# Making the stored copy of a turned tile on GpSimd instead of ScalarE, in a fused linear-attention and mixture-of-experts kernel

## The reference

```python
xn = _layernorm(x, axis=-1)
x = x + attn(xn) + ffn(xn)
# attn: q = xn@Wq, v = xn@Wv, s[t] = lam*s[t-1] + v[t], y = layernorm(q*s)*ln_g + ln_b
#       y = y * silu(xn@Wg), out = y@Wo
# ffn:  probs = softmax(xn@router.T), top 8 of 64 experts, at most 128 tokens an expert,
#       silu(xg@w1) * (xg@v1) @ w2, scaled by the weight and added to its tokens
```

## Time and profile before

| what | us |
|---|---|
| median of 3 runs | 2541.22 (2540.82 to 2541.46) |
| the profiled execution, its own time | 2539.86 |
| span of its trace | 2538.2 |
| PE busy | 2493.7 |
| DVE busy | 1629.1 |
| ACT busy | 1320.7 |
| POOL busy | 674.5 |

### The profile page before, as it was taken

One profiled execution on the slowest core, in us unless ns is written; L12 is line 12 of the kernel. 1 busy time (PEld: TensorE's weight loads), 2 busy tenths in 40 slices (PEclk: granted clock), 3 DMA queues, 4 the chain that ended last, 5 costly groups with the idle time before them and its releaser, 6 DMA issues.

```text
span 2538.2 us, 39295 instructions
## 1 busy us (share of the span) xinstructions
PE 2493.7 (98%) x13649; PEld 2214.3 (87%) x13649; DVE 1629.1 (64%) x1689; ACT 1320.7 (52%) x1499; POOL 674.5 (27%) x523
## 2 busy tenths in 40 slices
PE   7999999999999999999999999999999999999997
PEld 6888978898889988899888998889988889988896
DVE  7776897666666665666566666656666566656654
ACT  5566323554446644556445565445654456544554
POOL 3221122223322232322223222322223222323211
PEclk9999999999999999999999999999999999999999
DMA  8785854897668966779766797765986669866686
GB/s 278 260 301 193 240 189 162 257 306 228 191 224 254 312 215 217 228 234 295 239 228 204 227 316 249 224 217 197 311 277 191 224 217 284 276 217 228 207 268 162
DMA packets 151790, 605.74 MB, mean 239 GB/s; under 512 B 20592, under 2 KB 37040, under 8 KB 151216
## 3 DMA queue, kind: packets, MB, share of 16 engines
q1 hardware_dynamic: 116304, 518.91, 57.1%
q0 software_dynamic: 35424, 86.00, 16.5%
HBM read 520.89 MB, written 100.70 MB: 245 GB/s over the span
## 4 chain that ended last, share of the span: by engine, by line
PE 93%; DVE 3%; DMA 2%; ACT 1%; issue 1%; POOL 0%; SPq 0%; ACTq 0%; DVEq 0%; POOLq 0%
PE psA L1543 18%; PE psA L1545 18%; PE psA L1544 18%; PE psH L1543 7%; PE psH L1545 7%; PE psH L1544 7%; PE psY L1543 4%; PE psY L1545 4%; PE psY L1544 3%; PE psX L1650 2%; PE psY L1575 2%; PE psX L1670 1%; DMA ew_raw<-ew_dram 1%; DMA xn_turned<-xraw 1%; PE psH L1689 1%
## 5 line engine op out<-in xcount | busy, mean ns | idle before, releaser
L1156 DVE TENSOR_TENSOR ew_lo<-ew_raw,ew_hi 128x1536 fp32r<-128x1536 f32 x384 | 693.9, 1816 | 340.1 <-ACT ew_hi L752 326.0
L752 ACT ACTIVATE ew_hi<-ew_raw 128x1536 fp32r<-128x1536 f32 x384 | 568.4, 1484 | 163.0 <-DMA ew_raw<-ew_dram 128.5
L1543 PE MATMUL psA<-xT_hi,pw_hi 128*128 128x512 f32 (+1 forms) x1544 | 621.3, 402 | 3.5 <-DVE xT_lo L1073 2.9
L746 ACT ACTIVATE pw_hi<-pw_raw 128x1024 fp32r<-128x1024 f32 x254 | 266.4, 1060 | 674.2 <-PE psA L1545 671.7
L1545 PE MATMUL psA<-xT_hi,pw_lo 128*128 128x512 f32 (+1 forms) x1544 | 610.5, 395 | 0.0
L1544 PE MATMUL psA<-xT_lo,pw_hi 128*128 128x512 f32 (+1 forms) x1544 | 606.8, 393 | 0.0
L1151 DVE TENSOR_TENSOR pw_lo<-pw_raw,pw_hi 128x1024 fp32r<-128x1024 f32 x256 | 313.8, 1236 | 161.5 <-ACT pw_hi L746 156.1
L1543 PE MATMUL psH<-ew_hi,gT_hi 128*128 128x384 f32 x1024 | 352.7, 344 | 0.8
L1545 PEld LDWEIGHTS psA<-xT_hi,pw_lo 128*128 128x128 f32 x1544 | 292.4, 189 | 69.8
L1544 PEld LDWEIGHTS psA<-xT_lo,pw_hi 128*128 128x128 f32 x1544 | 294.9, 191 | 63.5
L1543 PEld LDWEIGHTS psA<-xT_hi,pw_hi 128*128 128x128 f32 x1544 | 291.5, 189 | 64.9 <-issue 4.7
(11 more groups left out here) (161 smaller groups left out, 3342.3 us busy)
## 6 DMA issues: line engine op xcount, KB each, us to landing
ew_raw<-ew_dram SPq DMA_DIRECT2D x384, 768.0 KB, 6.3
pw_raw<-proj_w_dram SPq DMA_DIRECT2D x256, 512.0 KB, 5.2
xn_scratch<-xt SPq DMA_DIRECT2D x33, 512.0 KB, 4.6
xt<-x_dram SPq DMA_DIRECT2D x32, 512.0 KB, 6.0
out_dram<-x_dram SPq DMA_DIRECT2D x32, 512.0 KB, 5.7
out_dram<-ot POOLq DMA_DIRECT2D x32, 512.0 KB, 12.4
xn<-xn_turned SPq DMA_DIRECT2D x29, 512.0 KB, 4.1
xn_turned<-xraw SPq DMA_DIRECT2D x28, 512.0 KB, 5.1
```

The lines of the kernel that those rows point to most:

```text
L746: act.activation(dst[:, slot, :, :], pw_raw[:, slot, :, :], ACT.Copy).then_inc(s_pwhi, 1)
L752: act.activation(ew_hi[:, c % 3, :], ew_raw[:, c % 3, :], ACT.Copy).then_inc(s_ewhi, 1)
L1156: dve.tensor_tensor(ew_lo[:, c % 3, :], ew_raw[:, c % 3, :], ew_hi[:, c % 3, :].bitcast(F32), ALU.subtract).then_inc(s_ewlo, 1)
L1543: pe.matmul(dst, l_hi, r_hi_, start=first, stop=False)
```

## The change

GpSimd gets `whole(k)`: it waits for `rt_lo` of tile k, and for the store of tile k-2, and adds the high and the low part into `xraw`. The raw copy on ACT is gone. `low` on DVE subtracts from the PSUM bank instead of `xraw`. The waits follow: ACT's rounded copy of tile k waits for the sum of tile k-2 (both read the same `rt_hi` buffer), and PE's turn of the last eight tiles waits for the low part of the tile before (the bank is read until then). The `z_lo` of block 0 and the sums of the last eight tiles alternate on GpSimd. SP's list is the same.

```diff
+            def whole(k):
+
+                if k >= NT + 2:
+                    wait_alone(pool, s_tst[k % 2], 16 * ((k - NT) // 2))
+                pool.wait_ge(s_plo, k + 1)
+                pool.tensor_tensor(xraw[:, k % 2, :, :], rt_hi[:, k % 2, :, :].bitcast(F32),
+                                   rt_lo[:, k % 2, :, :].bitcast(F32), ALU.add).then_inc(s_praw, 1)
...
                     if k % NT == 2:
                         inv_std(group_of(k) + 1)
+                    whole(k)
                 if p % 4 == 0 and p > 0:
                     add_sums(0, mm - 1, 1)
                 elif p % 4 == 2:
                     add_sums(0, mm, 0)
             add_sums(0, KC // 2 - 1, 1)
             inv_std_y(0)
-            inv_std(NB + 1)
-            for m in range(KC - 1):
-                z_lo_of(0, m)
+            for m in range(KC):
+                if m == 2:
+                    inv_std(NB + 1)
+                    z_lo_of(0, 0)
+                if m >= 2:
+                    z_lo_of(0, m - 1)
+                whole(NTILE - KC + m)
...
             def turned_hi(k):
                 act.wait_ge(s_pT, k + 1)
                 dst = xT_hi[:, :, k * P:(k + 1) * P] if k < NT else rt_hi[:, k % 2, :, :]
-                if k >= NT:
-                    if k >= NT + 2:
-                        wait_alone(act, s_tst[k % 2], 16 * ((k - NT) // 2))
-                    act.activation(xraw[:, k % 2, :, :], chunks(bank_of(k)), ACT.Copy).then_inc(s_praw, 1)
+                if k >= NT + 2:
+                    act.wait_ge(s_praw, k - NT - 1)
                 act.activation(dst, chunks(bank_of(k)), ACT.Copy).then_inc(s_phi, 1)
...
-                raw = chunks(bank_of(k)) if k < NT else xraw[:, k % 2, :, :]
-                dve.tensor_tensor(dst, raw, hi.bitcast(F32), ALU.subtract).then_inc(s_plo, 1)
+                dve.tensor_tensor(dst, chunks(bank_of(k)), hi.bitcast(F32), ALU.subtract).then_inc(s_plo, 1)
...
                 if k >= NTILE - KC:
-                    pe.wait_ge(s_phi, k)
-                    pe.wait_ge(s_plo, k - 1)
+                    pe.wait_ge(s_plo, k)
                 elif k >= NT:
                     pe.wait_ge(s_plo, k - 1)
```

## The result

| what | before | after |
|---|---|---|
| median of 20 runs each | 2537.66 us (2533.60 to 2541.95) | 2541.97 us (2538.66 to 2545.12) |
| profiled execution, its own time | 2539.86 | 2545.12 |
| span of its trace | 2538.2 | 2543.3 |

The ratio after to before is 1.0017, with a 95% interval of 1.0010 to 1.0024: 4.3 us longer, less than the 0.2% that was called no change. The forecast was 2545.2 us, range 2537.0 to 2550.0, and +4.0 us. It started from the median of three runs, 2541.22 us; over 20 runs the kernel before has 2537.66, so the forecast time is 3.2 us above the measured one although the difference is nearly right.

A forecast was written before the change was run, and what follows sets the result against it. PE, busy 98%, bounds the kernel; only idle gaps and low-clock stretches can be won. Terms +1.5 - 1.3 - 1.6 + 3.3 + 1.0 + 1.1 = +4.0 us on 2539.86, plus 1.36, give 2545.2 us, range 2537 to 2550.

The forecast's parts named there:

- The price of a sum: One GpSimd addition of 128x1024, 28 of them: 2.4 us each, 67 us in all, hidden as busy time.
- A: PE's 2.32 us idle gap before tile 8: whole(6) ahead of both sums costs 2.4, shorter chain gives 0.9, +1.5 us.
- B: PE's 1.29 us idle gap for `keys`: `keys` ready about 0.6 us before PE needs it, -1.3 us.
- C: PE's 1.62 us idle gap before tile 18: high part of tile 17 no longer waits for a store, -1.6 us.
- E: PE's 0.18 us idle gap before the token sums: whole(22), whole(23) and collisions delay them to about 188.6 us, +3.3 us.
- D: PE's 0.30 us idle gap at 176.6 us, which the prediction counted into E.
- F: PE's 2.10 and 1.38 us gaps at the stretch's end: 0.8 us won for k = 6, k = 7 later, +1.0 us.
- G: PE's 0.66 us idle gap at 339 us: last store issued later, DVE enters its saturated stretch late, +1.1 us.
- The clock: PE's granted clock in 20 us stretches: a 0.83 row costs 3.4 us; the sum of +4.0 us had only waiting.
- Rival two: "Another stretch at half clock" behind the late token sums: 3.4 us more, +7.4 us in all, 2548.6 us; chance 0.20.
- the locks miss: Rival: GpSimd and DVE collisions fall beside the chains; -7.6 us, 2533.6 us, or 2537.0 without the clock; chance 0.17.
- no change: Rival: what B and C give is what E and F take, the rest hidden; 2541.2 +- 1 us; chance 0.08.

The follow-up runs named there:

- Experiment 1: Changed kernel with GpSimd's whole(22) and whole(23) moved behind the last add_sums of the projections: 2533.17 us, ratio 0.9984 to the kernel before.
- experiment 3: Changed kernel with one wait more, GpSimd's whole(22) waiting for the nmr of tiles 24 to 27: 2540.64 us, ratio 1.0012 to the kernel before.
- experiment 5: Changed kernel with one wait more, GpSimd's whole(31) waiting for DVE's last low part lo_z7: 2543.81 us, ratio 1.0022 to the kernel before.
- experiment 2: Changed kernel with GpSimd's whole(6) moved behind rs and both add_sums of step p = 2, and waiting for nmr: 2536.19 us, ratio 0.9990.

## Why the prediction was right, and where it wasn't

**The verdict and the time held**, in part by luck: idle time rose by 2.2 us where the sum had +4.0, the clock, which the sum had at nothing, added some 4.6 us up to 280 us, and the two errors offset each other.

**The price of a sum** was 2.4 us on record and 2.40 in the trace. The guess by a memset's growth over size was good. The reading that two SBUF inputs exclude GpSimd held at every place named; it was too narrow, as the mask and the cast (one source) waited as well.

**A: +1.5 on record, +1.12 measured.** From the end of `rs` to the end of `nmr` the chain grew by 2.05 us (4.06 to 6.11), not 2.4: this half was off. The other half, 0.9 us from the copy that ACT no longer makes, was right, though `rs` came later, at 55.82 instead of 54.83 us. The low clock at the start had made everything late, PE too, which ran dry at 60.85 instead of 58.93 us. Against PE, `rs` is 0.93 us earlier, and 2.05 - 0.93 is the 1.12 us. In the kernels with the half sum and the copy, without that low clock, it came at 54.05 and 54.13.

**B and C: -1.3 and -1.6 on record, both gaps gone.** The raw copy with its wait for a store was their cause, as the late copy on ACT shows without any sum. The size of C, though, was one run's: it is 0.41 us in the second profile of the same kernel and 1.15 with the low part from PSUM.

**E: +3.3 on record, +2.84 of idle time**, or +2.54 with the 0.30 us of D, which the prediction counts in. The chain was told right step by step: `whole(22)` waited out `pw_lo`, `nmr` waited for `whole(22)`, and PE started at 188.48 us where 188.6 was forecast. The start agrees in part by accident, since PE itself came about 0.4 us later than before. Experiment 1 shows that the two sums are E, experiment 3 roughly how it divides.

**F: +1.0 on record, +0.52 measured.** The first gap fell by 0.84 us (0.8 on record), the second grew by 1.36 (1.8 on record). One `wt` ran ahead of the sum and the other waited it out, as foreseen.

**G: +1.1 on record, +1.19 measured in the first pair of profiles, +0.34 in the second** (0.68 to 1.02 us). That the last store works on G is shown by moving it (experiment 5); that the size was right is luck.

**The clock: 0 on record, +4.6 us up to 280 us.** This is the step that failed: the sum priced each gap as idle time alone. Rival two had the mechanism, "another stretch at half clock" with +3.4 us behind E, at a chance of 0.20. It came behind A (0.74 against 0.83) and E alike, in both profiles. Against the second profile of the kernel before, which has no low clock at E, E alone is 5.2 us worse. Of the total of +7.4 us that it forecast, +4.3 was measured, as idle time came out at +2.2 where the sum had +4.0. I had charged gaps as idle time and held the clock for an extra; in this kernel the two belong into one price.

**The rivals "the locks miss" and "no change"** are told by the same rows. At a sum of 2.4 us the locks don't miss; at 1.3 us the kernel is 3 us faster, not unchanged.

**What stays open** is the row from 20 to 40 us. In all seven profiles with whole sums on GpSimd throughout it has a granted clock of 0.91 to 0.95, in the seven others (two of them with a half sum or a copy in the sums' place) 1.00. That is too even to be put down to chance. Yet the first sum starts near 41 us, after the stretch, and the kernel with half sums, which still has two whole ones there, does not show it. I had expected it to change from run to run, and it did not. The low clock begins between 18.6 and 20 us, near the end of an idle gap that every kernel has before its first projection. The rows of PE, of the changed kernel and then of the one with the copy:

```profile
14.23 1.91 PE L1567 MATMUL psA<-ident,xt 128*128 128x128 f32 x8
...
19.76 0.55 PE L1553 MATMUL psA<-xT_hi,pw_hi 128*128 128x256 f32 x1 [2.69 <-DVE xT_lo L1083]
```

```profile
14.23 1.40 PE L1566 MATMUL psA<-ident,xt 128*128 128x128 f32 x8
...
19.25 0.36 PE L1552 MATMUL psA<-xT_hi,pw_hi 128*128 128x256 f32 x1 [2.73 <-DVE xT_lo L1082]
```

The gap is as long in both, and over all profiles its length does not part the two groups (1.81 to 2.90 us in the seven, 2.65 to 3.13 in the others). The turn of the third tile does: begun near 14 us, it takes 1.52 to 1.92 us in the seven and 1.04 to 1.49 us in the others. The eight transposes take 1.04 us at full speed, so in the seven PE came up to full speed later, and it fell back at the gap. The dividing line, between 1.49 and 1.52 us, is thin. The low clock there costs 1.7 us, 1.4 of them in this row, out of the 4.3 us. Why PE came up later in these kernels, no run here tells.

## What to carry to other kernels

An operation that GpSimd takes over is free as busy time and dear in its place: look at what stands behind it in GpSimd's list, and at each DVE operation that could fall into its length, and put it behind the last thing that somebody waits for. Moving three of 28 sums was worth 14 us; the plain alternative, a copy on ACT behind the step that the next tile needs, gave the same without GpSimd. And where PE idles for 2 us, count a half-clock stretch behind it with the gap: at A it cost 3.4 to 5.2 us, more than the gap itself. It is a risk and not a fixed price, as the gap at 19 us shows.

## What the runs showed of the hardware

- DVE operations with one SBUF source (a 128x256 mask, a 128x2048 cast from int32) waited for GpSimd's operation to end and held the next one off. The cast showed 2.31 to 2.33 us in every kernel, of which 1.08 us are work, as worked out in experiment 2.
- A GpSimd operation took 2.40 us for 128x1024 with two sources, 1.30 for 128x512, and 1.04 for a copy of 128x1024.
- Where both engines have an operation ready, they take turns: the sum, the mask, `y_sum`, the cast, `q_sum`, `nmr` at 57 to 63 us, each started where the other's ended.
- PE's low clock followed one and the same gap in one run and not in another (0.83 and 1.00 behind 0.18 and 0.19 us), which is worth 3.4 us. The two profiles of the kernel before are 6.5 us apart, and this and gap C (1.62 and 0.41 us) are 4.6 us of it.
- Whether the low clock followed the gap at 19 us went with how late PE had reached full speed before it, and not with the length of the gap: 2.69 us with it, 2.73 without.
